# Registers in batches, a ring of twelve blocks, and other places for norms and low halves

## The chip, the cores and the metric

The kernel runs on one core of one Trainium2 chip. The time is device microseconds of one execution, as a median of several runs. The core has TensorE (PE), VectorE (DVE), ScalarE (ACT), GpSimd (POOL) and SyncE (SP, which issues most DMAs).

## The reference

x is 16 batches of 128 tokens with 256 features. Two layers, each with an attention and a feed-forward part; every part takes a layer norm of x and is added to x with a gate:

```python
x = x + tanh(g_xattn[0]) * long_conv(norm(x), k, bias, ctx, ctx)          # stage A
x = x + tanh(g_ffn[0])   * moe_and_shared(norm(x), Wr, Wg, Wu, Wd, Sg, Su, Sd, Wsg)   # stage B
x = x + tanh(g_xattn[1]) * attention_16_heads(norm(x), ctx, ctx)          # stage C, causal
x = x + tanh(g_ffn[1])   * lora_moe(norm(x), ...)                         # stage D
# stage B, for each token: p = softmax(x @ Wr); the 2 best of 8 experts, weight p
#   sum over them of p_e * (silu(x @ Wg[e]) * (x @ Wu[e])) @ Wd[e]        # width 176
#   + sigmoid(x @ Wsg) * (silu(x @ Sg) * (x @ Su)) @ Sd                   # shared, width 704
```

## The kernel before

Every engine has its own program, written out by hand in order; an engine that waits for a semaphore holds everything behind it. Products of float32 are made of three float32r products: each operand is split into a high half (a ScalarE copy to float32r) and a low half (the difference), and high*high + high*low + low*high is summed in PSUM.

**Stage B, the shared expert.** Four groups of 512 tokens, six tiles of 128 hidden units each (the last tile has 64), numbered n = 0 to 23. For tile n TensorE makes the gate and up products (`b_gate_up`, L1946, 12 matmuls), ScalarE the silu (`b_silu_of`), VectorE the product h (`b_hidden`, L1400), ScalarE and VectorE the halves of h (`b_high`, `b_low`, L1405), and TensorE adds the down product (`b_down`, L1960) one or two tiles later. Before a new group the halves of its turned x are made (`b_high_x`, `b_low_x`, L1389). At the end of each tile, `b_side` puts other work on each engine:

- the routed experts' weights come in ten chunks: SyncE fetches chunk c when the low half of chunk c - 2 is made, ScalarE makes its high half (`experts_high`, L802) in tile c, GpSimd its low half (`experts_low`, L631)
- VectorE makes the norms of groups 1 to 3 in 38 small steps, 13 per tile; ScalarE applies them in tiles 3 to 5, four batches each (`b_norm`, L762)
- TensorE turns the normed x (L1897) and makes the router's logits; VectorE takes them (`logits_copy`), picks the experts (28 steps of `route_step`, from tile 9), and writes each token's slots (L1311); then it writes the table of blocks (`table_step`)

GpSimd scatters each token's row twice into `x_d` (L635, an indirect DMA for 128 rows), so that the rows of one expert lie together: eight scatters of group 0 between the low halves, 24 after the slots of groups 1 to 3 are written.

**Stage B, the blocks.** After tile 17, 39 blocks of 128 rows are run, each with one expert. SyncE reads the block's row from the table into a register and fetches it into a ring of six buffers (`block_in`, L468 and L469), four blocks ahead; it waits until the block that had the buffer is done. SyncE's program alternates `block_in(i + 4)` and `block_out(i)` (the store to `y_d`, L473). TensorE turns the block (`blk_turn`, L1996), reads the expert's offset into a register (L2001) and makes gate and up with it as a dynamic offset (L2009), reads another register (L2023) and makes the down product (L2030), and turns h (L2019, L2020). VectorE reads a third (L1470) for the column with the weight (L1474). Per step s TensorE's order is: turn of s + 1, gate and up of s, down of s - 2, turn of h of s - 1.

**Then** come tiles 18 to 23, beside which GpSimd gathers the blocks' results back into X (L641, 32 indirect DMAs with addition, eight per group of four batches).

**Stage C.** 32 steps (half the heads of one batch each). Per step: scores (L2065, mask L2069), VectorE's row maximum (L1495) and shift (L1505) in `c_shift`, ScalarE's exp (L887), turns (L2079), values. VectorE makes the norm of a later group in 23 steps between them; `rows_complete(g)` waits until group g's gathers have landed. In the kernel before, the norm of group 1 is made ahead of the first `c_shift`, that of group g + 2 in the steps of group g; ScalarE applies the norm of g + 1 in steps 0 to 3 (`c_norm_one`, L749), TensorE turns it in steps 4 to 7.

## Time and profile before

| | us |
|---|---|
| median of 3 runs | 894.62 |
| lowest, highest | 890.34, 896.23 |
| the profiled execution | 894.95 |
| its span, first to last instruction | 893.2 |

| engine | busy us | share of the span |
|---|---|---|
| TensorE, matmuls | 724.9 | 81% |
| VectorE | 577.9 | 65% |
| ScalarE | 309.4 | 35% |
| GpSimd | 256.0 | 29% |

The mean granted clock of TensorE is 0.92 of its full 2.4 GHz. The stages in the span: A to about 172, tiles 0 to 17 to about 291, blocks to about 436, tiles 18 to 23 to about 470, C to about 631, D to the end.

### The profile page before, as it was taken

To read this page: it belongs to the slowest core of one execution; us is meant where nothing else is said; L and a number is where in the kernel's file an instruction comes from. 1 tells how busy PE (TensorE), PEld (TensorE's weight loads), DVE (VectorE), ACT (ScalarE), POOL (GpSimd) and SP (SyncE) were. 2 spreads that over 40 slices of the span, in tenths; PEclk is the share of its full clock that TensorE was granted. 3 is DMA by queue.
4 is the path that set the end of the run, shared out by engine and by line. 5 is a ranking of instruction groups with operands and counts; after the bars stand their busy time and mean duration, and the time that the engine had idled before them with its cause. 6 is when DMAs were issued, how large, how long until landed. Compare 5 with 4: busy or idle time off the path is not lost.

```text
span 893.2 us, 13171 instructions
## 1 busy us (share of the span) xinstructions
PE 724.9 (81%) x4198; PEld 574.7 (64%) x4214; DVE 577.9 (65%) x1221; ACT 309.4 (35%) x539; POOL 256.0 (29%) x256
## 2 busy tenths in 40 slices
PE   2788888587978778877874888997769899999995
PEld 2565666476767656656662555665658788788884
DVE  5879888472356444444353778889457976877764
ACT  2110110154422222222232566875334335334231
POOL 1979777454447000000076810100100000000000
PEclk9999999797979899999995789998679999999997
DMA  8210100132213222222165512120010101001000
GB/s 271 71 50 27 36 24 1 48 95 74 70 56 140 67 78 68 73 73 77 42 110 98 81 50 82 54 85 2 1 47 1 48 25 48 1 24 48 23 1 24
DMA packets 42923, 51.25 MB, mean 57 GB/s; under 512 B 7088, under 2 KB 36976, under 8 KB 42224
## 3 DMA queue, kind: packets, MB, share of 16 engines
q1 hardware_dynamic: 36720, 41.98, 14.9%
q0 software_dynamic: 6144, 8.52, 4.8%
q8 instruction: 32, 0.52, 0.2%
q14 instruction: 27, 0.22, 0.1%
HBM read 36.88 MB, written 13.59 MB: 57 GB/s over the span
## 4 chain that ended last, share of the span: by engine, by line
PE 38%; DVE 16%; DMA 10%; issue 6%; POOL 5%; ACT 5%; SPq 2%; DVEq 0%; ACTq 0%; POOLq 0%
PE bank L2158 21%; DMA A<-x_d 4%; DMA X<-y_d,A 4%; PE bank L2009 3%; PE bank L1946 3%; POOL x_d L635 3%; DVE A L1505 3%; PE bank L2079 2%; DVE small L1495 2%; POOL X L641 2%; PE bank L2030 2%; ACT A L887 2%; PE bank L1996 1%; DMA A<-rows_d 1%; PE bank L2065 1%
## 5 line engine op out<-in xcount | busy, mean ns | idle before, releaser
L2158 PE MATMUL bank<-R 128*128 128x512 f32 (+3 forms) x1080 | 221.3, 365 | 22.4 <-DVE R L1617 6.4
L2158 PEld LDWEIGHTS bank<-R 128*128 128x128 f32 (+1 forms) x1080 | 183.2, 193 | 57.8 <-issue 8.3
L641 POOL DMA_INDIRECT X<-y_d,A x32 | 50.1, 1567 | 172.6 <-DMA y_d<-A 154.6
L1946 PE MATMUL bank<-R 128*128 128x512 f32 x264 | 74.4, 438 | 5.3 <-DVE R L1389 4.3
L1946 PEld LDWEIGHTS bank<-R 128*128 128x128 f32 x264 | 55.8, 218 | 17.5 <-issue 4.4
L2079 PE MATMUL bank<-ident,A 128*128 128x128 f32 x256 | 41.4, 314 | 30.4 <-ACT A L887 30.2
L2009 PE MATMUL bank<-R 128*128 x234 | 52.2, 362 | 13.4 <-issue 13.0
L1854 PE MATMUL bank<-A 128*128 128x256 f32 x128 | 43.2, 420 | 23.6 <-issue 12.4
L586 POOL TENSOR_TENSOR A<-A 128x256 f32<-128x256 f32 x64 | 58.0, 906 | 13.7 <-DVE A L1152 13.6
L2079 PEld LDWEIGHTS bank<-ident,A 128*128 128x128 f32 x256 | 33.4, 161 | 40.0 <-ACT A L887 25.4
L697 POOL TENSOR_TENSOR A<-A 128x512 f32<-128x512 f32 x4 | 5.2, 1288 | 180.1 <-DVE A L1611 180.1
L1152 DVE TENSOR_TENSOR A<-bank,A 128x512 f32<-128x512 f32 x64 | 43.7, 683 | 16.9 <-PE bank L1856 14.4
L1400 DVE TENSOR_TENSOR A<-bank,A 128x512 f32<-128x512 f32 (+1 forms) x24 | 16.5, 689 | 58.7 <-ACT A L785 58.7
L1960 PE MATMUL bank<-R 128*128 128x256 f32 (+1 forms) x288 | 43.1, 304 | 13.7 <-DVE R L1405 13.7
L1141 DVE TENSOR_TENSOR A<-A 128x512 f32<-128x512 f32 x64 | 52.9, 827 | 2.1 <-ACT A L723 2.1
L2009 PEld LDWEIGHTS bank<-R 128*128 128x128 f32 x234 | 40.2, 201 | 21.8 <-issue 21.7
L1960 PEld LDWEIGHTS bank<-R 128*128 128x128 f32 (+1 forms) x288 | 40.3, 207 | 17.5 <-DVE R L1405 14.1
L1642 DVE TENSOR_TENSOR A<-bank,A 128x512 f32<-128x512 f32 (+1 forms) x48 | 33.0, 688 | 28.0 <-PE bank L2158 27.5
L1854 PEld LDWEIGHTS bank<-A 128*128 128x128 f32 x128 | 21.1, 197 | 42.0 <-issue 40.9
L1495 DVE TENSOR_REDUCE small<-bank 128x8 f32<-128x1024 f32 x32 | 39.0, 1219 | 14.0 <-PE bank L2069 14.0
L591 POOL TENSOR_TENSOR A<-A 128x128 f32<-128x128 f32 x64 | 43.7, 683 | 14.1 <-PE bank L1866 9.3
L681 POOL TENSOR_TENSOR R<-A,R 128x960 f32 x8 | 18.4, 2299 | 100.2 <-ACT R L882 100.2
(274 smaller groups left out, 1376.3 us busy)
## 6 DMA issues: line engine op xcount, KB each, us to landing
A<-x_d SPq DMA_DIRECT2D x39, 132.0 KB, 2.0
y_d<-A SPq DMA_DIRECT2D x39, 128.0 KB, 1.7
A<-rows_d SPq DMA_DIRECT2D x4, 1024.0 KB, 4.6
A<-in_w SPq DMA_DIRECT2D x8, 480.0 KB, 3.7
A<-in_w SPq DMA_DIRECT2D x5, 512.0 KB, 3.8
A<-in_ctx_one SPq DMA_DIRECT2D x8, 272.0 KB, 3.6
A<-in_ctx_half SPq DMA_DIRECT2D x8, 256.0 KB, 2.7
A<-in_ctx_nat SPq DMA_DIRECT2D x4, 512.0 KB, 3.7
```

The costliest lines, as they stand in the source:

```text
L586: nc.gpsimd.tensor_tensor(zh[:, u], zr[:, u, :, 0:HALF, :], zr[:, u, :, HALF:, :], ALU.add).then_inc(zh_ready, 1)
L591: nc.gpsimd.tensor_tensor(z2[:, :, :, h * I0:(h + 1) * I0], zh[:, u, :, 0:QUARTER, :], zh[:, u, :, QUARTER:, :], ALU.add).then_inc(z2_read ...
L641: nc.gpsimd.indirect_dma_start(out=X[:, b], out_offset=None, in_=y_d[:, :], in_offset=bass.IndirectOffsetOnAxis(ap=y_slots[:, b, r:r + 1], ...
L1141: nc.vector.tensor_tensor(kv[:, u], vT[:, :, t0:t0 + I0].unsqueeze(3).to_broadcast([P, 8, I0, I0]), c.unsqueeze(2).to_broadcast([P, 8, I0, ...
L1152: nc.vector.tensor_tensor(zr[:, u], yb[u].rearrange("p (q i j) -> p q i j", q=8, i=I0), c.unsqueeze(3).to_broadcast([P, 8, I0, I0]), ALU.m ...
L1495: step.mark(nc.vector.tensor_reduce(mx[:, u], S, AX_X, ALU.max))
L1854: nc.tensor.matmul(y[:, 0:n], diag, kv0, start=True, stop=False, skip_group_check=True)
L1946: mm = nc.tensor.matmul(dst, wX[:, a0:a0 + P], mX[:, k], start=(m == 0), stop=(m == 5))
L1960: mm = nc.tensor.matmul(DN[:, b * D:(b + 1) * D], hX[0:pr, n % 2, b * P:(b + 1) * P], wX[0:pr, a0:a0 + D], start=(j == 0 and m == 0 and b ...
L2009: mm = nc.tensor.matmul(GU[i % 2][:, 0:2 * EF], xX[:, i % 2, k * P:(k + 1) * P], w[:, k, :, :, bass.ds(at, RANK)], start=(m == 0), stop=(m ...
L2079: mm = nc.tensor.transpose(PTP[:, h * P:(h + 1) * P], E_[:, k % 2, h], ident[:])
L2158: mm = nc.tensor.matmul(dst, a, m, start=start and n == 0, stop=stop and n == len(prods) - 1, skip_group_check=skip)
```

## The change

- All values of the table that one engine needs in the blocks are read into registers ahead of the stage, in two loads (20 and 19 values). One table of experts, used with a factor, takes the place of three tables. The check of bounds at each read is left out.
- The ring of blocks has twelve buffers, where the rows to scatter lay before; fetches run eight blocks ahead.
- In tiles 0 to 9 VectorE makes the low halves of the routed weights. GpSimd only scatters, and begins with group 0 at once.
- VectorE finishes the norm of groups 1 to 3 in tile 2; ScalarE applies it in tiles 2 to 6, two or three batches each.
- At the end of a group the halves of h are made before those of the next x, on ScalarE and VectorE; in tile 5 the copy of the turned x comes before the silu; the logits of group 1 are taken before `b_finish`; in tile 11 no routing steps lie before the halves.
- Stage C starts without the norm of group 1. The norm of g + 1 is made in the steps of group g: from step 2 in group 0, from step 0 in the others, done in step 3. ScalarE applies it in steps 3 to 6.

```diff
@@ -72,6 +72,11 @@
 TURN_AT = (4, 5, 6, 7)
+REGS_PER_LOAD = 20
+XB = 12
+AHEAD = 8
+NORM_AT = (2, 0, 0)
+NORMS_IN = {2: (4, 5), 3: (6, 7, 8), 4: (9, 10), 5: (11, 12), 6: (13, 14, 15)}
@@ -205,7 +210,7 @@
         bsilu, bh = (A1[:, 10240 + i * 512:10240 + (i + 1) * 512].rearrange("p (u n) -> p u n", u=2) for i in range(2))
-        xb = [A1[:, 11264 + i * XROW:11264 + (i + 1) * XROW] for i in range(6)]
+        xb = [A1[:, i * XROW:(i + 1) * XROW] for i in range(XB)]
...
@@ -333,7 +339,7 @@
             sem("down_done"), sem("b_done"))
-        blk_loaded, y_stored = [sem(f"blk_loaded{i}") for i in range(6)], [sem(f"y_stored{i}") for i in range(4)]
+        blk_loaded, y_stored = [sem(f"blk_loaded{i}") for i in range(XB)], [sem(f"y_stored{i}") for i in range(4)]
@@ -378,6 +384,17 @@
+        def table_values(engine, view, top):
...
+            values = []
+            for lo in range(0, NBLK, REGS_PER_LOAD):
+                hi = min(lo + REGS_PER_LOAD, NBLK)
+                _, got = nc.values_load_multi_w_load_instructions(
+                    view[0:1, lo:hi], [engine], min_val=0, max_val=top,
+                    skip_runtime_bounds_check_because="the table's entries are bounded where it is made")
+                values.extend(got)
+            return values
@@ -456,27 +473,24 @@
                 sp.dma_start(x_d[bass.ds(at, P), :], zeros).then_inc(rows_zeroed, 16)
+            row_at = table_values(mybir.EngineType.SP, trow, X_ROWS - P)
...
             def block_in(i):
-                if i < 6:
-                    if i < 4:
-                        sp.wait_ge(xsL_ready, NCHUNK)
-                else:
-                    sp.wait_ge(y_made, i - 5)
-                at = sp.value_load(trow[0:1, i:i + 1], min_val=0, max_val=X_ROWS - P)
-                sp.dma_start(xb[i % 6], x_d[bass.ds(at, P), :]).then_inc(blk_loaded[i % 6], 16)
+                if i >= XB:
+                    sp.wait_ge(y_made, i - XB + 1)
+                sp.dma_start(xb[i % XB], x_d[bass.ds(row_at[i], P), :]).then_inc(blk_loaded[i % XB], 16)
...
             def block_out(i):
...
-            for i in range(4):
+            for i in range(AHEAD):
...
             for i in range(NBLK):
-                if i + 4 < NBLK:
-                    block_in(i + 4)
+                if i + AHEAD < NBLK:
+                    block_in(i + AHEAD)
@@ -625,11 +639,6 @@
-            def experts_low(c):
-                pool.wait_ge(xsH_ready, c + 1)
-                h, l, src = expert_chunk(c)
-                nc.gpsimd.tensor_tensor(l, src, h.bitcast(F32), ALU.subtract).then_inc(xsL_ready, 1)
@@ -643,13 +652,9 @@
-            experts_low(0)
-            experts_low(1)
-            for c in range(2, NCHUNK):
-                experts_low(c)
-                if c == 2:
-                    pool.wait_ge(slots_ready, 1)
-                scatter((c - 2) // 2, (c % 2,))
+            pool.wait_ge(slots_ready, 1)
+            for b in range(BG):
+                scatter(b)
@@ -805,9 +810,8 @@
                     experts_high(n)
-                if 3 <= n < 6:
-                    for b in range(BG):
-                        b_norm(BG * (n - 2) + b)
+                for b in NORMS_IN.get(n, ()):
+                    b_norm(b)
@@ -816,13 +820,13 @@
             def b_group(g):
...
                     n = SJ * g + j
-                    b_silu_of(n)
...
                         b_turned(1)
+                    b_silu_of(n)
+                    b_high(n - 1)
...
                         b_high_x(g + 1)
-                    b_high(n - 1)
@@ -933,10 +937,10 @@
                         c_exp(g + (k + 2) // 8, (k + 2) % 8)
-                    if more and k < BG:
-                        if k == 0:
+                    if more and 3 <= k < 3 + BG:
+                        if k == 3:
                             act.wait_ge(qT_turned, BG * (g + 1))
-                        c_norm_one(g + 1, k)
+                        c_norm_one(g + 1, k - 3)
@@ -1367,21 +1371,17 @@
                 elif i == 14:
-                    step.mark(nc.vector.tensor_scalar(tcol, te_, float(D), None, ALU.add))
+                    nc.vector.tensor_copy(tcol, te_).then_inc(table_ready, 1)
                 elif i == 15:
-                    step.mark(nc.vector.tensor_scalar(t16, te_, float(RANK), None, ALU.mult))
+                    step.mark(nc.vector.tensor_tensor(tdelta_, tcum_, tblk_, ALU.subtract))
                 elif i == 16:
-                    nc.vector.tensor_scalar(t256, te_, float(D), None, ALU.mult).then_inc(table_ready, 1)
-                elif i == 17:
-                    step.mark(nc.vector.tensor_tensor(tdelta_, tcum_, tblk_, ALU.subtract))
-                elif i == 18:
...
                 else:
-                    y_slot_step(i - 19)
+                    y_slot_step(i - 17)
...
             def block_table():
-                return Steps(table_step, 25)
+                return Steps(table_step, 23)
@@ -1425,10 +1425,21 @@
+            def experts_low(c):
+                dve.wait_ge(xsH_ready, c + 1)
+                if c >= 8:
+                    dve.wait_ge(pads_zeroed, 4)
+                h, l, src = expert_chunk(c)
+                nc.vector.tensor_tensor(l, src, h.bitcast(F32), ALU.subtract).then_inc(xsL_ready, 1)
...
             def b_side(n, norm, route, table):
+                if n == 2:
+                    norm.take_all()
                 norm.take(13)
-                if n in (6, 7, 8):
+                if n in (7, 8):
                     logits_copy(n - 5)
+                if n < NCHUNK:
+                    experts_low(n)
@@ -1438,13 +1449,13 @@
                     b_hidden(n)
-                    if j == SJ - 1 and g + 1 < G:
-                        b_low_x(g + 1)
-                    if n >= 9:
+                    if n >= 9 and j < SJ - 1:
...
                     b_low(n - 1)
+                    if j == SJ - 1 and g + 1 < G:
+                        b_low_x(g + 1)
@@ -1465,16 +1476,18 @@
+            expert = []
...
             def blk_out(i):
...
-                col = dve.value_load(tcol[0:1, i:i + 1], min_val=D, max_val=D + E - 1)
...
                     dve.wait_ge(y_stored[i % 4], 16 * (i // 4))
-                nc.vector.tensor_scalar(yo[i % 4], DB[i % 2][:, 0:D], xb[i % 6][:, bass.ds(col, 1)], None, ALU.mult
+                nc.vector.tensor_scalar(yo[i % 4], DB[i % 2][:, 0:D], xb[i % XB][:, D:].rearrange("p (e n) -> p e n", n=1)[:, bass.ds(expert[i], 1), 0], None, ALU.mult
...
             def blocks():
+                expert.extend(table_values(mybir.EngineType.DVE, tcol, E - 1))
@@ -1526,20 +1539,22 @@
             def c_steps(g, more):
                 norm = Steps()
-                if g + 2 < G:
-                    rows_complete(g + 2)
-                    norm = c_norm(BG * (g + 2), BG * (g + 3))
...
                 for k in range(8):
+                    if more and k == NORM_AT[g]:
+                        rows_complete(g + 1)
+                        norm = c_norm(BG * (g + 1), BG * (g + 2))
...
                         norm = d_norm(BG, B - BG)
-                    norm.take(3 if more else 6)
+                    norm.take((3, 3, 8, 8)[k % 4] if more and g == 0 else 3 if more else 6)
+                    if more and k == 3:
+                        norm.take_all()
@@ -1759,11 +1774,14 @@
             norm.take(8)
+            experts_low(0)
...
                     b_hidden(SJ * (g + 1))
+                if g == 0:
+                    logits_copy(1)
@@ -1783,14 +1801,9 @@
             nc.vector.memset(OT, 0.0).then_inc(ot_zeroed, 1)
-            rows_complete(1)
-            norm = c_norm(BG, 2 * BG)
-            norm.take(4)
             c_shift(0, 0)
-            norm.take(3)
-            c_shift(0, 1, norm)
-            c_shift(0, 2, norm)
-            norm.take_all()
+            c_shift(0, 1)
+            c_shift(0, 2)
@@ -1988,17 +2001,18 @@
+            expert = []
...
             def blk_turn(i):
-                pe.wait_ge(blk_loaded[i % 6], 16 * (i // 6 + 1))
+                pe.wait_ge(blk_loaded[i % XB], 16 * (i // XB + 1))
...
                 for k in range(DT):
-                    mm = nc.tensor.transpose(XT[i % 2][:, k * P:(k + 1) * P], xb[i % 6][:, k * P:(k + 1) * P],
+                    mm = nc.tensor.transpose(XT[i % 2][:, k * P:(k + 1) * P], xb[i % XB][:, k * P:(k + 1) * P],
...
             def blk_gate_up(i):
-                at = pe.value_load(t16[0:1, i:i + 1], min_val=0, max_val=(E - 1) * RANK)
@@ -2007,7 +2021,7 @@
                         mm = nc.tensor.matmul(GU[i % 2][:, 0:2 * EF], xX[:, i % 2, k * P:(k + 1) * P],
-                                              w[:, k, :, :, bass.ds(at, RANK)], start=(m == 0), stop=(m == 5))
+                                              w[:, k, :, :, bass.ds(expert[i] * RANK, RANK)], start=(m == 0), stop=(m == 5))
@@ -2020,7 +2034,6 @@
             def blk_down(i):
-                at = pe.value_load(t256[0:1, i:i + 1], min_val=0, max_val=(E - 1) * D)
@@ -2028,12 +2041,14 @@
                         mm = nc.tensor.matmul(DB[i % 2][:, 0:D], hX[:, i % 2, a0:a0 + P],
-                                              w[:, bass.ds(at, D)], start=(m == 0), stop=(m == 5))
+                                              w[:, bass.ds(expert[i] * D, D)], start=(m == 0), stop=(m == 5))
...
             def blocks():
                 pe.wait_ge(table_ready, 1)
+                pe.wait_ge(xsL_ready, NCHUNK)
+                expert.extend(table_values(mybir.EngineType.PE, tcol, E - 1))
```

## Rows read from the trace of the kernel before

**Rows 1.** Stretches of the span: us, busy by engine, TensorE's clock, DMA share, GB/s.

```profile
172.00:255.00 83.00, 65.91 (x338) 56.77 (x338) 40.93 (x103) 38.88 (x59) 34.47 (x26) 0.83 0.25 77
...
292.00:299.00 7.00, 5.91 (x21) 5.07 (x22) 1.62 (x4) 1.79 (x5) 0.00 (x0) 0.52 0.29 77
299.00:436.00 137.00, 107.37 (x600) 83.33 (x599) 61.30 (x151) 39.35 (x112) 0.00 (x0) 0.97 0.23 70
```

**Rows 2.** Timeline of TensorE, tiles: start, us, instruction, idle before.

```profile
196.41 2.73 PE L1960 MATMUL bank<-R 128*128 128x256 f32 x12 [2.65 <-DVE R L1405]
...
207.17 2.93 PE L1960 MATMUL bank<-R 128*128 128x256 f32 x12 [3.65 <-DVE R L1405]
...
218.27 1.94 PE L1897 MATMUL bank<-ident,A 128*128 128x128 f32 x8 [1.95 <-DVE A L1247]
...
247.51 0.22 PE L1916 MATMUL bank<-A 128*128 128x96 bf16 x1 [2.11 <-DVE A L1273]
...
275.23 1.60 PE L1960 MATMUL bank<-R 128*128 128x256 f32 x12
...
279.41 1.60 PE L1960 MATMUL bank<-R 128*128 128x256 f32 x12
```

**Rows 3.** One line's durations (min/median/max ns), then timeline of GpSimd and VectorE.

```profile
L1087 DVE TENSOR_TENSOR A<-A x3: 170/172/2785, 191.5 to 196.5; 128x12 f32<-128x12 f32 x3
...
192.54 2.37 POOL L631 TENSOR_TENSOR R<-A,R 128x1024 fp32r<-128x1024 f32 x1
...
195.67 0.68 DVE L1405 TENSOR_TENSOR R<-A,R 128x512 fp32r<-128x512 f32 x1
```

**Rows 4.** Slots written, the scatters by line, the first block's turn.

```profile
254.48 0.18 DVE L1311 CAST A<-A 128x24 int32<-128x24 f32 x1
...
L635 POOL DMA_INDIRECT x_d<-A x32: 959/964/2449, 191.3 to 286.7; - x32
...
292.07 0.52 PE L1996 MATMUL bank<-ident,A 128*128 128x128 f32 x2 [3.15 <-DMA A<-x_d]
```

**Rows 5.** Timeline of TensorE in the blocks, gate products.

```profile
294.30 2.12 PE L2009 MATMUL bank<-R 128*128 x6 [0.37 <-issue]
...
299.09 1.25 PE L2009 MATMUL bank<-R 128*128 x6
...
301.57 1.27 PE L2009 MATMUL bank<-R 128*128 x6
...
430.03 1.26 PE L2009 MATMUL bank<-R 128*128 x6 [0.25 <-issue]
```

**Rows 6.** Register loads by line: all, then one of 416:418; timeline of TensorE.

```profile
L2001 PEldq TENSOR_LOAD <-A x39: 296/302/563, 293.2 to 429.2; - x39
...
L2023 PEldq TENSOR_LOAD <-A x1: 303/303/303, 417.1 to 417.1; - x1
...
416.70 1.27 PE L2009 MATMUL bank<-R 128*128 x6 [0.41 <-issue]
```

**Rows 7.** Waits of 300:430: total us, times, longest.

```profile
PE bank L1996 <- DMA A<-x_d: 12.3, 17, 1.4
```

**Rows 8.** Timeline at the attention: first scores, then VectorE.

```profile
472.99 0.63 PE L2069 MATMUL bank<-neg,identb 128*128 128x512 bf16 x1 [0.33 <-issue]
...
483.31 1.41 DVE L1062 BATCH_NORM_STATS2 A<-X 128x6 f32<-128x256 f32 x4 [13.02 <-DMA X<-y_d,A]
...
498.82 1.08 DVE L1062 BATCH_NORM_STATS2 A<-X 128x6 f32<-128x256 f32 x3 [0.32 <-DMA X<-y_d,A]
...
499.82 1.21 DVE L1495 TENSOR_REDUCE small<-bank 128x8 f32<-128x1024 f32 x1
...
537.82 1.21 DVE L1495 TENSOR_REDUCE small<-bank 128x8 f32<-128x1024 f32 x1
...
571.26 1.22 DVE L1495 TENSOR_REDUCE small<-bank 128x8 f32<-128x1024 f32 x1
...
602.73 1.19 DVE L1495 TENSOR_REDUCE small<-bank 128x8 f32<-128x1024 f32 x1
```

11 lines of the change are left out of this document (6 added, 5 removed).

## The prediction

> **What bounds the kernel now.** I read the table of stretches first [rows 1]. TensorE is busy nearly all of the last stage, which the change doesn't touch. Three stretches leave room. In 172 to 255 (tiles 0 to 11 of the shared expert) its granted clock is 0.83 of 2.4 GHz on average. In 299 to 436 (39 blocks) TensorE is busy 107 of 137 us at 0.97. At 470 the attention starts late.
>
> The timeline of the tiles [rows 2] shows TensorE waiting for VectorE before the down products of tiles 2 and 4, before the turn of group 2's rows and before the ranks: 2.65 + 3.65 + 1.95 + 2.11 = 10.4 us. A tile without waits takes 4.18 (275.23 to 279.41). One reason lies in [rows 3]: a step of the norm on 128x12 values took 2.79 us where the same line takes 0.17 at other times, and GpSimd's low half of 2.37 us ran from 192.54 beside it.
>
> What ends the tiles isn't TensorE. The last slots are written at 254.66; then GpSimd issues 24 scatters until 287.66, 1.36 us apart on average; the last lands, the first block is fetched, and its turn starts at 292.07 after a wait of 3.15 [rows 4]. So what counts here is when the slots are ready; the 37.4 us behind them are one queue.
>
> In the blocks [rows 5] the gate products start 294.30, 299.09 (two later), 301.57, and last 430.03: 38 intervals in 135.7 us, 3.57 each, while the interval 299.09 to 301.57 is 2.48. The waits [rows 7] name 12.3 us before the turns for the fetch. Another part is the register load: TensorE's queue takes 0.30 us to read a value, twice per block [rows 6].
>
> In the attention VectorE sat 13.02 us until 483.31 for the gathered rows of group 1, though the first scores were there at 473.6, and the fourth reduction came at 499.82 after a second wait for group 2, which ended at 498.82 [rows 8].
>
> **The tiles.** Ten low halves go from GpSimd (2.37 us each) to VectorE. VectorE's own difference of 128x512 takes 0.68 [rows 3], so one of 128x1024 is about 1.2, and ten are 11.6 us (nine of 1.2, one of 0.68; the trace shows none of this size on VectorE; at the rate of the 0.68 row the bounds are 1.1 and 1.36 each). They stand at the end of a tile's VectorE work, where it has some 2 us of slack against a tile of 4.18, except where norm steps stand too. I followed the queues with the durations of the trace:
> - The 10.4 us of TensorE's waits go, with two causes: GpSimd no longer stops VectorE, and the halves of h come before the halves of x.
> - Waits come back: 1.0 before the down of tile 0 (a low half in front of the second hidden tile), 1.5 before that of tile 2 (ScalarE now waits for the whole norm in tile 2 with the next silu queued behind it), 2.3 before that of tile 4 (norms 9 and 10 and the copy of the turned x stand ahead of the silu). Sum 4.8. Net 5.6.
> - With fewer gaps some of the 1.2 GHz stretches end. At 0.83 over 83 us about 14 us were at the low level, which costs up to 7 us of TensorE time if it is all in matmuls; I take 3.4, half.
> So the slots are ready 9.0 us earlier (between 4, if a wait more is left and the clock stays, and 13). The chain of chunk loads (fetch waits for a low half two chunks back, then the high half, then the low half) takes about 1.2 + 4 + 1.1 us in two tiles of 4.2 and stays hidden; if it didn't, each tile would cost 1 to 2 us.
>
> The 24 scatters keep their 33 us. The eight of group 0 now come before, beside the first tiles, and hold nobody. SyncE's registers for the fetches are read while it waits for the scatters, 0.5 us off the path (its first value was read between the last landing and the fetch). The zeroing of pads, 15 transfers, waits for the table, which moves earlier with the tiles and is then done 5 to 10 us ahead of the scatters. Tiles 12 to 17 end before the scatters, so the changes there give nothing. First block 9.5 us earlier. TensorE then idles longer before it, and starts at 1.2 GHz as now (0.52 in 292 to 299), which I keep.
>
> The Trainium skill, "GPSIMD Engine Reference" (Specifications), says that GpSimd's SBUF interfaces are shared with VectorE, with contention when VectorE has two SBUF inputs. By that rule, the trace agrees [rows 3], and it also speaks against the change: the low halves have two such inputs and now lie beside the eight early scatters. By the rule those would be late by up to 10 us, in a stretch where nothing waits for them, so the sum stays.
>
> **The blocks.** Per block three register loads go (two on TensorE's queue, one each on VectorE's and SyncE's) and are replaced by two batches per engine ahead of the stage; those on TensorE and SyncE stand in front of waits that last anyway, VectorE's stand before the first low half of a block, while the scatters still run. I cost them at nothing; no row shows a load of 20 registers, and if 39 values last as 39 single ones (39 x 0.30 = 11.7 us), VectorE, which has some 7 idle before the first block, costs 5, so 0 to 5. The load of 20 is nearer to one instruction, so I take 0.
> The ring of twelve with fetches eight ahead asks for a block that ended three blocks ago; a fetch takes 2.1 us plus issue, and no wait remains. What is left is the array: gate products 1.25, down products about 0.83, four turns of 0.11 apart. That is the 2.48 of [rows 5], of which there is only one sample. Dependences: from the turn of h over ScalarE (0.38) and VectorE (0.43) to the down product are 1.3 us, where the turn and gate products of the next block give 1.7. ScalarE's 1.1 and VectorE's 1.7 us of work in a block don't bind. I take 2.52 (bounds 2.48, and 2.9, the interval of undelayed blocks now). First two intervals 4.8 as before, 36 x 2.52 = 90.7, and 2 for stretches at half clock: 97.5 against 135.7, gain 38.2 (with 2.9: 24.6; with no half clock and 2.48: 41.6).
>
> The Trainium skill, "TensorE: Matmul & The Clock Gate" (Step-by-step), says that the sequencer spends about 62 ns on each matmul. What TensorE's queue did is seen in [rows 6]: gate products began at 416.70, and the next register load started at 417.1, with twelve instructions (weight loads and matmuls) between: some 33 ns each. At 62 ns for weight loads and matmuls alike, a block of 32 would be 2.0 us plus address operations and waits of 0.6, so an interval of 2.6 and 3 us less gain. The trace doesn't agree, and I stay with 2.52.
>
> **The attention.** The norm of group 1 leaves the start. The first reduction can begin at 473.6 and not 484.6, 11.0 earlier, and the fourth no longer waits for group 2: 1.4 more. Rows of group 1 land at 483.3, when VectorE reaches them after some 487; group 2 at 498.7 against 505 or later; group 3 some 20 us early. So none of these waits is due. Put back: from the fourth reduction of a group to that of the next were 33.4 us with a norm of a later group inside and 31.5 without [rows 8]; the last group now gets one: 2.0. ScalarE's norms wait in step 3 for the end of VectorE's steps, in group 0 for eleven of them, 2.2 us with 1 of cover; next is the copy of turned p: 1.2. Net 9.2, bounds 4 and 12.4.
>
> **Sum.** The profiled execution took 894.95 (span 893.2 and 1.75 around); the median is 894.62, the same within 0.04%. 894.95 - 9.5 - 38.2 - 9.2 = 838.
>
> **Rivals.**
> A. The blocks stay near 2.9 because a dependence or the queue's order binds and not the load: gain 24.6 there, 852. For it: only one interval of 2.48. Against: the 1.3 against 1.7 above. Chance 0.18.
> B. The tiles give nothing, since VectorE's 11.6 us take what GpSimd's stalls cost: 838 + 9 = 847. Chance 0.12.
> C. Norm steps inside the attention are exposed one by one (23 steps of 0.2 in each of three groups, 14 us): 838 + 9 = 847. Chance 0.1.
> D. Slower: the longer idle before the blocks holds TensorE at 1.2 GHz through them. At that clock an interval is up to 2 x 2.48 = 4.96, 2.44 over mine. The gain of 56.9 is gone when 23 of 38 intervals are so; all of them give 838 + 93 = 931. For it: the clock was 0.52 in 292 to 299 and the tiles of 172 to 255 ran at 0.83. Against: it rose after 7 us, and the blocks will have fewer gaps than those that ran at 0.97. Chance 0.03.
> E. The change doesn't do what it says: fetches or loads still hold the blocks (a batch that stands in the way, or a fetch queued behind a store): 850 to 862. Chance 0.07.
> The forecast itself: 0.5.
>
> **Range.** The corners of the bounds are 829 and 864; 827 to 856 leaves out most of E, D and the worst corner. A measurement tells about 1% from no change, 9 us. Faster by over 1%: 0.95; within 1%: 0.01; slower: 0.04.
>
> **What would show it.** Starts of the gate products 2.5 apart with no wait for a fetch; no small norm step of over 2 us in the tiles; slots ready about 245.5 and the first turn about 282.5, still one queue of scatters between; the first reduction of the attention some 3 us after its memset and no wait for a gather of over 2 us after it. The prediction is wrong if VectorE becomes what tiles wait for, if intervals of blocks stay over 2.8, or if TensorE's clock in the blocks is under 0.9.

## The result, and the profile after

The changed kernel took 825.07 us in the median of four runs (817.5 to 830.01) beside 892.94 for the kernel before (890.34 to 896.23): a ratio of 0.921, 95% interval 0.912 to 0.930. The ratios here leave out the few executions that ran in the chip's slower state, among them the one of 830.01. The profiled execution took 828.8 (span 827.1, mean clock 0.928), 66.1 us under the 894.95 of before; 838 was forecast.

Where the 66.1 us come from, by the starts of the same instructions in both traces: 12.9 until the first block's turn (forecast 9.5; 0.5 of it lies ahead of the tiles); 50.8 from there to the last block's gate products (38.2); 1.8 from there to the last reduction of the attention (9.2); 0.6 behind it.

Stretches of the changed kernel (us, busy time by engine, TensorE's clock, DMA share, GB/s), to be held against [rows 1]:

```profile
172.00:255.00 83.00, 71.45 (x416) 61.52 (x417) 54.85 (x142) 41.32 (x64) 20.93 (x25) 0.96 0.29 92
...
299.00:360.00 61.00, 61.00 (x435) 57.91 (x434) 42.81 (x109) 26.48 (x82) 0.00 (x0) 1.00 0.40 117
```

In the tiles the clock is 0.96 where it was 0.83; in the blocks TensorE is never shown idle, at full clock.

The tiles and the queue behind them, from timelines of TensorE and GpSimd, against [rows 2, 4]:

```profile
185.84 1.67 PE L1973 MATMUL bank<-R 128*128 128x256 f32 x12 [0.99 <-DVE R L1405]
...
195.96 1.70 PE L1973 MATMUL bank<-R 128*128 128x256 f32 x12 [1.45 <-DVE R L1405]
...
203.23 1.70 PE L1973 MATMUL bank<-R 128*128 128x256 f32 x12 [1.88 <-DVE R L1405]
...
235.02 0.22 PE L1929 MATMUL bank<-A 128*128 128x96 bf16 x1 [2.66 <-DVE A L1277]
...
242.20 1.15 POOL L644 DMA_INDIRECT x_d<-A  x1 [56.87 <-DVE A L1315]
...
279.22 1.09 PE L2011 MATMUL bank<-ident,A 128*128 128x128 f32 x4 [10.06 <-DMA A<-x_d]
```

Three waits before down products are 0.99, 1.45 and 1.88, as followed (1.0, 1.5, 2.3); the fourth, before the ranks, didn't go (2.66, was 2.11). The scatters start at 242.20, were 254.93, and their queue is as long as before.

One block of the changed kernel, all engines (timeline, weight loads left out):

```profile
292.14 1.23 PE L2023 MATMUL bank<-R 128*128 x6
292.20 0.38 ACT L852 ACTIVATE R<-bank 128x256 fp32r<-128x256 f32 x1 [0.75 <-PE bank L2034]
...
292.62 0.42 DVE L1476 TENSOR_TENSOR R<-bank,R 128x256 fp32r<-128x256 f32 x1
...
293.21 0.62 PE L2043 MATMUL bank<-R 128*128 x3
...
294.02 0.27 PE L2033 MATMUL bank<-ident,A 128*128 128x128 f32 x1
...
294.24 0.38 PE L2011 MATMUL bank<-ident,A 128*128 128x128 f32 x2
...
294.37 0.41 PE L2023 MATMUL bank<-R 128*128 x1
```

The interval is 2.23 here (292.14 to 294.37) and 2.24 over the stage; the first starts are 280.97, 283.17 and 285.39, the last 366.36, against [rows 5]. The busy time of the six gate products is 1.23, yet the down products begin 1.07 after them: the busy time holds the tail of the last matmul, beneath which the next ones already start.

The batches of register loads (one line, by queue: count, min/median/max ns, first and last start), where [rows 6] had one load per value:

```profile
L392 SPq TENSOR_LOAD <-A x2: 4566/4704/4842, 263.8 to 268.6; - x2
L392 PEldq TENSOR_LOAD <-A x2: 4928/5435/5942, 267.6 to 273.6; - x2
L392 DVEq TENSOR_LOAD <-A x2: 4441/4915/5389, 269.2 to 274.6; - x2
```

A batch of 20 or 19 values lasts 4.4 to 5.9 us, 0.24 to 0.28 a value over both, little less than the 0.30 of a single load [rows 6]. They are hidden: SyncE's end at 273.2, ahead of the last landing of the scatters at 276.7; TensorE's second begins at 273.6, and as the pair of durations fits only with the longer one first, it ends at 278.5, 0.7 before the turn.

In the attention the reductions (L1508) stand at 408.47 (484.63 before), 423.02, 460.93, 498.79 and 535.95 for the first and the fourth of each group, against [rows 8]; the last is at 557.32 (622.77 before). The start came 76 us earlier, of which groups 1 to 3 gave back 11.4. The chain of waits in steps 5 and 6 of group 0 shows with what:

```profile
450.85 1.06 ACT A L891
451.90 0.49 ACT A L754
...
452.44 0.44 PE bank L2125 x2
452.88 0.87 PE bank L2094 x8
```

After the exponential (L891) ScalarE computes a norm (L754), TensorE turns the normed rows (L2125), and only then p (L2094). Three steps in a row with this link are 4.08 to 4.13 us apart; in the kernel before the steps at the same place are 3.49, 3.87 and 3.49 apart.

### The profile page after: what moved, and what is told of

It is laid out like the page before. It is cut to its first block, busy times and chain, and to the rows that moved or that the text cites. A ratio compares the mean times of both kernels' runs of the same rounds, so it can differ in the third digit from the quotient of the medians.

```text
span 827.1 us, 12725 instructions
## 1 busy us (share of the span) xinstructions
PE 699.6 (85%) x4214; PEld 564.3 (68%) x4214; DVE 577.7 (70%) x1229; ACT 306.2 (37%) x539; POOL 233.1 (28%) x246
## 4 chain that ended last, share of the span: by engine, by line
PE 49%; DVE 16%; ACT 6%; issue 5%; POOL 3%; DMA 2%; DVEq 0%; ACTq 0%; SPq 0%
PE bank L2173 22%; PE bank L2023 5%; PE bank L2043 4%; PE bank L1959 4%; POOL x_d L644 3%; PE bank L2094 3%; PE bank L2080 2%; DVE A L1518 2%; DVE small L1508 2%; ACT A L891 2%; PE bank L2105 1%; PE bank L1973 1%; DVE A L1066 1%; DMA A<-rows_d 1%; PE bank L2011 1%
## 5 line engine op out<-in xcount | busy, mean ns | idle before, releaser
L2173 PEld LDWEIGHTS bank<-R 128*128 128x128 f32 (+1 forms) x1080 | 183.4, 193 | 56.9 <-issue 7.4
L650 POOL DMA_INDIRECT X<-y_d,A x32 | 50.3, 1571 | 119.0 <-DMA y_d<-A 101.8
L1959 PE MATMUL bank<-R 128*128 128x512 f32 x264 | 66.7, 404 | 5.3 <-DVE R L1389 4.3
L600 POOL TENSOR_TENSOR A<-A 128x256 f32<-128x256 f32 x64 | 58.8, 919 | 12.4 <-DVE A L1156 12.3
L1959 PEld LDWEIGHTS bank<-R 128*128 128x128 f32 x264 | 50.0, 195 | 15.5 <-issue 4.4
L1508 DVE TENSOR_REDUCE small<-bank 128x8 f32<-128x1024 f32 x32 | 39.1, 1220 | 28.2 <-PE bank L2084 28.2
L2094 PE MATMUL bank<-ident,A 128*128 128x128 f32 x256 | 41.8, 317 | 13.3 <-ACT A L891 13.3
L644 POOL DMA_INDIRECT x_d<-A x32 | 34.1, 1065 | 66.2 <-DVE A L1315 56.9
L1657 DVE TENSOR_TENSOR A<-bank,A 128x512 f32<-128x512 f32 (+1 forms) x48 | 33.0, 688 | 28.0 <-PE bank L2173 27.6
L2023 PE MATMUL bank<-R 128*128 x234 | 50.2, 353 | 0.7 <-DVE R L1464 0.7
L1867 PEld LDWEIGHTS bank<-A 128*128 128x128 f32 x128 | 20.6, 193 | 42.2 <-issue 41.4
L2094 PEld LDWEIGHTS bank<-ident,A 128*128 128x128 f32 x256 | 35.2, 165 | 20.8 <-ACT A L891 17.7
L993 ACT ACTIVATE A<-bank 128x512 f32<-128x512 f32 (+1 forms) x48 | 28.6, 595 | 52.8 <-PE bank L2173 52.6
L686 POOL TENSOR_TENSOR R<-A,R 128x960 f32 x8 | 18.4, 2299 | 100.6 <-ACT R L886 100.6
L1973 PE MATMUL bank<-R 128*128 128x256 f32 (+1 forms) x288 | 39.4, 286 | 7.6 <-DVE R L1405 7.5
L2080 PE MATMUL bank<-A 32*128 32x256 f32 x256 | 43.8, 467 | 2.1 <-issue 2.1
```

The lines of the kernel that those rows point to most:

```text
L600: nc.gpsimd.tensor_tensor(zh[:, u], zr[:, u, :, 0:HALF, :], zr[:, u, :, HALF:, :], ALU.add).then_inc(zh_ready, 1)
L644: nc.gpsimd.indirect_dma_start(out=x_d[:, :], out_offset=bass.IndirectOffsetOnAxis(ap=slots[:, b, r:r + 1], axis=0), in_=row_of(b), in_off ...
L650: nc.gpsimd.indirect_dma_start(out=X[:, b], out_offset=None, in_=y_d[:, :], in_offset=bass.IndirectOffsetOnAxis(ap=y_slots[:, b, r:r + 1], ...
L1508: step.mark(nc.vector.tensor_reduce(mx[:, u], S, AX_X, ALU.max))
L1867: nc.tensor.matmul(y[:, 0:n], diag, kv0, start=True, stop=False, skip_group_check=True)
L1959: mm = nc.tensor.matmul(dst, wX[:, a0:a0 + P], mX[:, k], start=(m == 0), stop=(m == 5))
```

## The experiments

Thirteen runs, each of two to six executions. "Blocks" is the time from the start of the first gate product of the first block to that of the last gate product of the last block (136.7 before, 86.3 after); an interval is the distance between the first gate products of two blocks in a row. For the attention three times are given: from the last gate product to the fourth reduction, then from there to that of group 1, and from that to the last reduction of all. Ratios are to the kernel before as run beside each, with 95% intervals (its medians were 889.23 to 894.8).

| kernel | median us | ratio | blocks | attention |
|---|---|---|---|---|
| before | 892.94 | | 136.7 | 68.8, 38.0, 85.0 |
| changed | 825.07 | 0.921 (0.912, 0.930) | 86.3 | 55.7, 37.9, 96.4 |
| changed_again | 826.26 | 0.928 (0.923, 0.933) | 86.3 | 56.0, 43.2, 93.6 |
| attention_old | 822.33 | 0.925 (0.920, 0.930) | 86.5 | 65.5, 37.0, 84.7 |
| attention_mixed | 814.31 | 0.915 (0.911, 0.920) | 86.4 | 55.3, 42.4, 84.8 |
| low_on_gpsimd | 830.38 | 0.934 (0.929, 0.940) | 86.8 | |
| ring_of_six | 851.02 | 0.959 (0.953, 0.966) | 104.7 | |
| load_per_block | 853.44 | 0.958 (0.951, 0.966) | 108.1 | |
| four_gate_products | 828.24 | 0.932 (0.924, 0.940) | 85.1 | |
| mixed_and_vector_low | 816.8 | 0.917 (0.912, 0.922) | 86.3 | 55.9, 42.2, 85.0 |
| low_wait_late_four | 813.0 | 0.911 (0.907, 0.915) | 69.7 | |
| low_wait_late | 825.98 | 0.924 (0.919, 0.928) | 82.5 | |
| halves_as_before | 834.51 | 0.936 (0.932, 0.941) | 86.2 | |
| norms_together | 829.67 | 0.928 (0.923, 0.933) | 86.4 | |
| mixed_and_late_wait | 813.1 | 0.910 (0.906, 0.914) | 82.4 | 53.4, 44.7, 84.6 |

The ratios of changed_again and of the changed kernel in the first row differ by 0.7 points: that is how much two groups of runs of the same kernel can differ.

### The blocks: fetches and loads

**changed_again**, the changed kernel beside the others.

> The changed kernel itself, so that the variants of this call have a measure on the same chip. Expected: 820 to 828 us, gate products of the blocks 2.24 apart, steps of the attention 4.13 apart where ScalarE's norm lies in front of a turn.

**ring_of_six.**

```diff
-XB = 12
-AHEAD = 8
+XB = 6
+AHEAD = 4
```

> The changed kernel with a ring of six buffers and fetches four blocks ahead, registers still read in batches. Theory 1 (the ring alone has a price of its own): a fetch is issued when block i is done and stored, 0.4 us, lands 2.1 later and is due two steps on, which asks for steps of about 2.7 us; intervals of 2.65 to 2.85, time 16 to 23 us above the changed kernel. Theory 2 (the register loads were what made fetches late, so a ring of six is enough without them): intervals of 2.24 to 2.3, within 4 us.

24.8 us slower than the changed kernel, somewhat over theory 1; 18.4 us of it lie in the blocks, an interval of 2.73. The chain of waits repeats this every 5.45 us, two blocks:

```profile
324.96 0.50 DVE A L1486
...
325.48 0.33 SPq L487
...
325.99 2.07 DMA A<-x_d
...
328.11 0.44 PE bank L2011 x2
328.55 1.04 PE bank L2023 x6
329.58 0.72 PE bank L2043 x6
```

VectorE scales the output (L1486), SyncE stores it (L487), only then issues the next fetch, which lands after 2.07; then turn, gate and down products lead to the next output. Between them the fetch and its place in SyncE's queue are a ring of two blocks. With eight ahead it is slack: in the changed kernel no turn after the first waits for a fetch.

**load_per_block.** The batches are gone; each engine reads its value in the block that uses it (one table of experts, so an address operation more than before).

```diff
-                expert.extend(table_values(mybir.EngineType.PE, tcol, E - 1))
...
             def blk_gate_up(i):
+                at = pe.value_load(tcol[0:1, i:i + 1], min_val=0, max_val=E - 1)
...
             def blk_down(i):
+                at = pe.value_load(tcol[0:1, i:i + 1], min_val=0, max_val=E - 1)
```

> The changed kernel with a register load per use again on TensorE, VectorE and SyncE, but the ring of twelve. Theory 1 (my step of 2.48 for the array held hidden load time; TensorE's queue is what binds with loads): intervals of 2.7 to 2.9 with no wait for a fetch, 18 to 25 us above the changed kernel. Theory 2 (loads are hidden under matmuls once no fetch is late): intervals of 2.24 to 2.48, 0 to 9 us above.

27.2 us slower, 21.8 of it in the blocks, an interval of 2.8 to 2.9, also a little over theory 1. TensorE's timeline:

```profile
327.69 1.27 PE L2023 MATMUL bank<-R 128*128 x6 [0.15 <-issue]
329.01 0.63 PE L2044 MATMUL bank<-R 128*128 x3
...
330.62 0.43 PE L2023 MATMUL bank<-R 128*128 x1 [0.18 <-issue]
```

In this block, from gate to down products are 1.32 in place of 1.07, and from there to the next gate products 1.61 in place of 1.16. Of these 0.70 us only 0.15 and 0.18 are shown as idle: the rest lies beneath the tails of matmuls that count as busy. Taken back alone, the ring costs 18.4 and the loads cost 21.8, which is 40.2 of the 50.4 us won in the blocks. So the two gains overlap: some 10.2 us are there as soon as either of the two is made, and are lost only when both are taken back.

### The blocks: what is left

**four_gate_products** leaves out the two products with the low half of x in each block's gate and up.

```diff
-                for xX, wX in ((bxH, guH), (bxH, guL), (bxL, guH)):
+                for xX, wX in ((bxH, guH), (bxH, guL)):
```

> The changed kernel without the products of the low half of x in the blocks' gate and up (four matmuls of six; that part of the sum is left out). Theory 1 (the array sets the interval of 2.24): 2 x 0.18 less, 1.88, 14 us faster. Theory 2 (the way of h over ScalarE and VectorE to the down product sets it): the interval stays above 2.1.

The interval stayed at 2.24 in this stretch (2.23 over the stage), so the array alone doesn't set it. The timeline (all engines, weight loads left out):

```profile
291.51 0.91 PE L2023 MATMUL bank<-R 128*128 x4
291.57 0.39 ACT L852 ACTIVATE R<-bank 128x256 fp32r<-128x256 f32 x1 [1.07 <-PE bank L2034]
...
291.99 0.42 DVE L1476 TENSOR_TENSOR R<-bank,R 128x256 fp32r<-128x256 f32 x1
...
292.57 0.63 PE L2043 MATMUL bank<-R 128*128 x3 [0.15 <-DVE R L1476]
...
293.51 0.27 PE L2034 MATMUL bank<-ident,A 128*128 128x128 f32 x1
...
293.81 0.38 ACT L852 ACTIVATE R<-bank 128x256 fp32r<-128x256 f32 x1 [1.04 <-PE bank L2034]
```

A ring: the turned h is copied (291.57), its low half made (291.99), the down products wait for it (292.57), the next h is turned behind them (293.51) and copied at 293.81, which is 2.24 after 291.57. The order of TensorE's queue closes it: turn h(i+1) stands behind down(i).

**low_wait_late_four and low_wait_late** cut that ring: the last two of six down products alone need the low half, and the wait is moved to stand in front of them.

```diff
             def blk_down(i):
-                pe.wait_ge(bhL_ready, i + 1)
+                pe.wait_ge(bhH_ready, i + 1)
...
                 for hX, w0_, w1_ in ((bhH, dH0, dH1), (bhH, dL0, dL1), (bhL, dH0, dH1)):
+                    if hX is bhL:
+                        pe.wait_ge(bhL_ready, i + 1)
```

> The changed kernel, but the down products wait for h's low half only before the last two of their six (the first four need the high half alone), and the gate and up products of a block leave out the two with the low half of x. With four gate products and the wait ahead of all six down products the interval stayed at 2.24 us. Theory 1 (a ring holds it there: copy of the turned h on ScalarE 0.39, low half on VectorE 0.43, down products and the next turn of h 1.0 to 1.2, with 0.15 to 0.2 between): with the wait later the ring is some 0.5 us shorter, TensorE alone is left, and the interval falls by the two products, 2 x 0.18, to 1.88 (gain 13 us in 38 intervals). Theory 2 (something outside that ring, a fetch or VectorE's turn with the output, gives the beat): the interval stays at 2.24.

> The changed kernel with that later wait alone, all twelve products there. Theory 1 (TensorE's own work, 1.08 for the gate products, 0.81 for the down products and 0.35 for four turns, is 2.24 as well, so that ring and engine are level): interval 2.24, time within 2 us of the changed kernel. Theory 2 (the ring alone gave 2.24 and TensorE's own work is less): the interval falls to 2.1 or below, 5 us or more faster.

With four gate products the interval falls to 1.81 and the time by some 15 us: theory 1. The chain is TensorE alone:

```profile
327.69 0.67 PE bank L2023 x4
328.36 0.71 PE bank L2045 x6
329.07 0.11 PE bank L2033
329.18 0.11 PE bank L2034
329.29 0.22 PE bank L2011 x2
```

With all twelve products the interval is 2.15 (gate products at 327.42 and 329.57), so the engine alone needs 0.09 less than the ring held it to. That is between the two theories: the interval lies nearer to the second (2.1) than to the first (2.24), while the median, 0.3 us under that of changed_again, is as the first has it. The 3.8 us that the trace shows in the blocks are too few for the medians to tell.

### The tiles

**low_on_gpsimd** gives the ten low halves back to GpSimd, in the old order among the scatters.

```diff
+            for c in range(2, NCHUNK):
+                experts_low(c)
...
-                if n < NCHUNK:
-                    experts_low(n)
```

> The changed kernel with the low halves of the routed weights back on GpSimd and everything else of the change kept. Theory 1 (the two engines hold each other up): steps of the norm of over 2 us come back, the whole norm is late, ScalarE waits for it in tile 2, slots ready 3 to 6 us later than in the changed kernel, time 3 to 6 us above it, since the scatters set the start of the blocks. Theory 2 (the reordered halves of h gave the gain of the tiles): within 1.5 us of the changed kernel.

**halves_as_before.** ScalarE's side of the end of a group; VectorE's likewise. The routing steps and, in tile 5, the silu stand in the old order too.

```diff
-                    b_high(n - 1)
                     if j == SJ - 1 and g + 1 < G:
                         act.wait_ge(gu_ready, n + 1)
                         b_high_x(g + 1)
+                    b_high(n - 1)
```

> The changed kernel, but in the shared expert's tiles ScalarE and VectorE make the halves of x for the next group ahead of those of h again, the routing steps stand in the last tile of a group as before, and the silu stands ahead of the copy of the turned rows. Low halves on VectorE and spread norms stay. Theory 1 (the order was one of the two causes of TensorE's waits, 2.65 us before the down products of tile 2 and 3.65 before those of tile 4 in the kernel before): waits of 2 to 4 us return before the down products at the ends of the groups, and the slots are ready 3 to 6 us later. Theory 2 (what was won came from GpSimd's low halves and from the spread norms): the slots are ready within 1 us of the changed kernel's.

**norms_together.**

```diff
-                for b in NORMS_IN.get(n, ()):
-                    b_norm(b)
+                if 3 <= n < 6:
+                    for b in range(BG):
+                        b_norm(BG * (n - 2) + b)
...
-                if n == 2:
-                    norm.take_all()
```

> The changed kernel, but the twelve norms of ScalarE stand in tiles 3, 4 and 5 in fours as before, and VectorE takes 13 norm steps per tile without finishing them in tile 2. Theory 1 (the norms were a part of the waits: four of them, some 2 us, ahead of ScalarE's next silu): the waits before the down products of tiles 3 to 5 grow to 2 to 4 us each in place of 1.0, 1.5 and 1.9, the slots are ready 3 to 5 us later. Theory 2 (in the tiles the spread norms give nothing, since VectorE must now end its steps in tile 2): the slots are ready within 1 us, or earlier.

The traces are compared from the start of the 36 gate products of the first tiles (174.50 before, 174.03 after), in us to the first late scatter and to the first block's turn: before 80.4 and 117.6; changed 68.2 and 105.2; changed_again 67.4 and 103.9; low_on_gpsimd 68.8 and 105.7; halves_as_before 69.7 and 110.8; norms_together 69.0 and 105.6. Against the mean of the two changed runs each part undone alone puts the slots 1.0, 1.9 and 1.2 later, in each case under the 3 us and more of theory 1. That is 4.1 of 12.6. The other 8.5 either stay as long as some of the parts are there or belong to one that no run takes back (the logits of group 1, taken earlier); no run takes two parts back together, so this stays open. In norms_together the waits of TensorE in question are 1.11 and 2.71, where theory 1 had 2 to 4 each. (The 4.1 us by which the median of low_on_gpsimd is slower meets its theory 1, but only 1.1 of it is there at the first turn.)

What the three don't give back is the low clock: in 172 to 255 it is 0.83 before, 0.96 in the changed kernel, and 0.94, 0.92 and 0.94 with one part undone. In the order of halves the waits did return (3.21 and 3.48 before down products), and the table comes late enough that the batches stand on the path. The chain of waits:

```profile
267.93 4.86 SPq L392
272.82 4.04 SPq L392
277.09 2.06 DMA A<-x_d
279.16 2.60 issue
281.76 0.68 PE bank L2011 x2
```

SyncE's two loads hold the first fetch until 277.09, and TensorE's own, the second of which starts at 277.1, hold the turn 2.60 longer. So the first turn comes 6.2 later with slots only 1.9 later, most of the 7.5 us that the ratios show.

In low_on_gpsimd a step of the norm was held again. GpSimd and VectorE beside each other (timeline):

```profile
186.51 2.40 POOL L645 TENSOR_TENSOR R<-A,R 128x1024 fp32r<-128x1024 f32 x1 [1.30 <-ACT R L816]
186.65 2.28 DVE L1088 TENSOR_SCALAR A<-A 128x12 int32<-128x12 int32 x1
```

The small step ends with GpSimd's operation: 188.93 and 188.91. A second one, of 2.25 us, ends at 229.68 with GpSimd's at 229.56. The step of 2.79 us in [rows 3] was of this kind (it ended at 194.95, GpSimd's operation at 194.91), and it was one of three in the tiles of the kernel before: the others took 2.38 from 188.72 and 2.25 from 240.80. With two of the three back, the slots were only 1.0 later.

### The attention

**attention_old** has the order of the kernel before there, all else changed.

```diff
+            rows_complete(1)
+            norm = c_norm(BG, 2 * BG)
...
-                    if more and k == NORM_AT[g]:
-                        rows_complete(g + 1)
-                        norm = c_norm(BG * (g + 1), BG * (g + 2))
...
-                    if more and 3 <= k < 3 + BG:
+                    if more and k < BG:
```

> The changed kernel with the attention's schedule as before (norm of group 1 first, norm of group g + 2 in the steps of group g, ScalarE's norms in steps 0 to 3). Theory 1 (the new places of ScalarE's norms and turns cost nearly what the early start gives, 12.9 us won and 11.4 lost): 1 to 3 us slower than the changed kernel, with 33 and 31.5 us between fourth reductions of groups 1 to 2 and 2 to 3 instead of 37.9 and 37.2. Theory 2 (the longer groups come from TensorE's clock or the DMAs of that execution and not from the schedule): 10 to 13 us slower than the changed kernel, with 37 to 38 us per group in both.

3.9 us faster in the median, with intervals of the ratios that overlap: the new order of the attention gives nothing, and perhaps costs. The groups are those of theory 1 (33.2 and 31.5 us for groups 1 and 2), but it had expected a slower kernel. The start is 10 us later and the groups behind group 0 are 84.7 in place of 93.6 to 96.4. The three times add up to 187.2, against 192.8 in changed_again and 190.0 in the changed kernel's own trace; the two differ by group 0 above all (43.2 and 37.9), for a reason that comes below.

**attention_mixed** keeps the early start and puts the norms back where they are cheap.

```diff
+                    if g == 0 and k == 2:
+                        rows_complete(1)
+                        norm = c_norm(BG, 2 * BG)
+                    if g == 0 and k == 5:
+                        rows_complete(2)
+                        norm = c_norm(2 * BG, 3 * BG)
+                    if g == 1 and k == 0:
+                        rows_complete(3)
+                        norm = c_norm(3 * BG, 4 * BG)
...
+                    at = 3 if g == 0 else 0
+                    if more and at <= k < at + BG:
```

> The changed kernel with the late norm of group 1 kept, but the norm of group 2 begun in step 5 of group 0 and ScalarE's norms of groups 2 and 3 in steps 0 to 3, away from the turns of q in steps 4 to 7. Theory 1 (ScalarE's norm, 0.50 us, is in the ring of exp, norm, turn of q, turn of p, copy when it lies in the same steps as the turn): 8 to 10 us faster than the changed kernel, 811 to 818 us, groups of 33.4 and 31.5. Theory 2 (VectorE's norm steps or the clock make the groups long): within 3 us of the changed kernel.

12 us faster than changed_again; the later groups took 84.8 again. The run moves VectorE's norms as well as ScalarE's, so it shows what the order costs, and not which of the two engines makes it so.

Two causes beside the link over ScalarE can be read from the traces. Group 2 took 37.2 us in the changed kernel at a clock of 0.91, 35.5 in changed_again at 1.00 and 31.5 in attention_mixed at 1.00. So 1.7 us go with the lower clock of one execution, and 4.0 with the order. Of these 4.0 the three steps with the link over ScalarE give 1.5. The others lie in the steps ahead of them, where the chain of waits holds VectorE's norm too (changed_again):

```profile
509.34 0.99 DVE A L1093
...
510.35 0.17 DVE A L1088
```

Group 0 took 42.4, though, and one step of VectorE in it shows why in part:

```profile
446.63 4.99 POOL L686 TENSOR_TENSOR R<-A,R 128x960 f32 x2
...
447.88 3.78 DVE L1513 TENSOR_SCALAR small<-small 128x8 f32<-128x8 f32 x1
```

The step on 128x8 values, 0.17 us elsewhere, ends at 451.66, GpSimd's pair of low halves at 451.62.

**mixed_and_vector_low** makes those low halves on VectorE too.

```diff
-                for r in range(2):
-                    split_low1(g, r)
...
+                        nc.vector.tensor_tensor(w1L[:, n * W1C:(n + 1) * W1C], stg1[k // 4],
```

> The kernel with the mixed attention schedule, and the eight low halves of the last stage's weights (128x960) on VectorE in steps 2 and 6 of each group, not on GpSimd. Theory 1 (a low half on GpSimd stops VectorE for up to 3.8 us in a step, and the gap drops TensorE's clock): no VectorE step of over 2 us in the attention, groups 1 to 4 us shorter in spite of 1.15 us more per half on VectorE, 2 to 8 us faster than the mixed schedule. Theory 2 (VectorE is in the ring of every step, and 9.2 us more work costs as much as the stalls): within 3 us of it, or slower.

No small step is held, and nothing is won: 816.8, group 0 42.2. VectorE pays for the low halves itself.

**mixed_and_late_wait** joins the edit of attention_mixed with the later wait in the blocks.

> The changed kernel with the mixed order of the attention's norms (the time 814.31 us alone) and the later wait for h's low half in the blocks (an interval of 2.15 in place of 2.24 us). Theory 1 (the two are apart, and the 42.4 us that group 0 of the attention took in the profile of the mixed order were the 3.8 us step of VectorE beside GpSimd's low halves, which falls differently when the stage begins 3 us earlier): the blocks give 3.4 us, 811 us in the median; group 0 takes 38 to 39 us if no small step of VectorE takes over 2 us, and over 41 only where one does. Theory 2 (the mixed order itself makes group 0 long, and its gain is in the later groups alone): group 0 takes over 41 us without any such step, and the median is still 811 to 815.

813.1 us, the fastest full kernel, 1.8 points of the ratio under changed_again; the blocks took 82.4. Group 0 took 44.7 with a held step:

```profile
438.00 4.97 POOL L686 TENSOR_TENSOR R<-A,R 128x960 f32 x2
...
438.78 4.23 DVE L1513 TENSOR_SCALAR small<-small 128x8 f32<-128x8 f32 x1
```

The changed kernel itself took 37.9 in group 0 without such a step and 43.2 with one of 3.18 (443.20 to 446.38, where GpSimd's operation ran to 446.35). The other runs with the order of the changed kernel say the same: with held steps of this kind of 1.62, 2.39, 3.04, 4.51 and 4.60 us group 0 took 39.1, 39.7, 41.7, 44.3 and 44.6, and with 0.8 or less 38.2, 37.8 and 37.8 (in the order low_on_gpsimd, norms_together, four_gate_products, load_per_block, low_wait_late; ring_of_six, low_wait_late_four, halves_as_before). So the step accounts for most of it, as theory 1 has it. The 42.2 of mixed_and_vector_low had none; two low halves on VectorE explain some 2.4 of that, an estimate by the 1.21 us that one of 128x1024 takes. What the mixed order by itself does to group 0 stays open.

## Why the prediction was off

The direction and the places were right, and all three terms were mis-sized: the blocks gave 12.6 us more than forecast and the tiles 3.4 more, the attention gave 7.4 less. That the total is off by only 9.2 in the profiled execution is luck, as the errors partly cancel. The median fell 2 us under the range of 827 to 856; the profiled 828.8 lies in it, and changed_again's median of 826.26 just under it. By the prediction's own bounds the corners are 827.5 and 861.9 (866.9 with the batches' 5), and not 829 and 864.

**The blocks: 50.3 against 38.2 between the gate products, the step that failed.** The forecast took the array as what is left, which is nearly so, but it mis-sized its work. It took "gate products 1.25, down products about 0.83, four turns of 0.11 apart" for it, 2.52 us a block; the starts give 2.14. Busy times of pipelined groups hold a tail that the next group hides. TensorE's timeline of before had the answer in the starts:

```profile
299.09 1.25 PE L2009 MATMUL bank<-R 128*128 x6
300.17 0.52 PE L2030 MATMUL bank<-R 128*128 x3
...
300.89 0.27 PE L2019 MATMUL bank<-ident,A 128*128 128x128 f32 x1
...
301.10 0.38 PE L1996 MATMUL bank<-ident,A 128*128 128x128 f32 x2
```

1.08 + 0.72 + 0.21 and 0.13 for the turn of x (294.24 to 294.37 after) are 2.14; low_wait_late measured 2.15. The sample of 2.48 was no measure of the array: between 301.10 and the gate products at 301.57 are 0.47, so it had a register load in it, which the forecast both counted as gone and kept in the sample. The ring over ScalarE and VectorE was looked at and dismissed ("1.3 us, where the turn and gate products of the next block give 1.7"). The 1.7 holds the same tail: from the turn of h at 294.02 to the down products at 295.45 are 1.43, and the way over the two engines, whose low half ends at 295.28, takes as long. So the ring binds at 2.24, and cost 3.8 us. The 12.1 us between the gate products are then 36 x 0.27 = 9.8 for the interval, 2.0 for half clock that wasn't needed (0.50 in 281 to 285, 1.00 from 285 to 367) and 0.4 for the first two intervals (4.4 in place of 4.8). Rival A (2.9) fell: no interval is so long once both the loads and the short ring are gone. The interval of 2.6 worked out in the prediction for 62 ns on weight loads and matmuls alike didn't come: in the chain of low_wait_late_four the two turns of h, a weight load and a matmul each, are 0.11 apart, 55 ns an instruction. The Trainium skill, "TensorE: Matmul & The Clock Gate" (Step-by-step), gives the 62 ns for matmuls, and only where the hardware decoder is off, which no run here tells; the trace doesn't agree that weight loads cost as much, and for matmuls alone it doesn't tell.

**The batches: cost nothing, for another reason.** "The load of 20 is nearer to one instruction" is wrong: 39 values take 9.4 to 10.9 us, near the pessimistic end of 11.7. They are hidden since the tables are ready early, on TensorE by only 0.7 us; with halves_as_before the cover is gone, and they hold the first block.

**The tiles: 12.9 against 9.5, mis-sized.** The waits that come back were 0.99, 1.45 and 1.88 as followed; that before the ranks stayed. So the waits gave some 3.4 net (10.4 less 7.0) and not 5.6. The clock gave more: "at 0.83 over 83 us about 14 us were at the low level" takes the time lost for the stretch at the low level. With half speed there, a mean of 0.83 is 28 us at the low level and 14 lost; at 0.96 it is 3.3 lost. Up to 10.8 could come back, where 3.4 was taken. That the clock gave the rest is worked out and not shown by a run of its own: the slots came 12.2 earlier after the start of the tiles, of which the waits explain 3.4, and the twelve down products that took 2.73 and 2.93 us behind the long waits [rows 2] took 1.67 to 1.70 after. Rival B (the tiles give nothing) fell: low halves of 128x1024 take 1.21 on VectorE, as estimated.

The Trainium skill, "GPSIMD Engine Reference" (Specifications), says that the interfaces to SBUF are shared with VectorE and that instructions in a 2-port mode or with two SBUF inputs contend. The traces agree, with more in them: a held step on 128x8 or 128x12 values lasts until GpSimd's operation ends, to within 0.04 us in five of the cases above. Whether the held steps with one input in SBUF run in a 2-port mode, no trace here shows. The prediction feared up to 10 us for the eight early scatters. Only one of them lay beside a low half on VectorE: it took 1.03 us in the changed kernel and 1.53 in changed_again, where 0.96 is usual.

**The attention: 1.8 against 9.2, mis-sized.** The start gave 13.1 (from the last gate product to the fourth reduction 68.8 and 55.7; forecast 12.4). Put back were 11.4 in the groups, not 3.2. The forecast priced "ScalarE's norms wait in step 3" once; it didn't see that in steps 3 to 6 they lie between the exponential and the turn of p each time: groups 1 and 2 took 37.9 and 37.2 us between their fourth reductions, where [rows 8] have 33.4 and 31.5. attention_old and attention_mixed show that the order does it; that the norms of ScalarE have a part is read from the chain of waits (1.5 us of the 4.0 in group 2 of changed_again). Rival C, VectorE's norm steps, was right for another part: they stand on the chain in the steps before, at times held by GpSimd. Rivals D and E didn't occur: the clock in the blocks is 1.00 after their first 4 us, and no fetch after the first was waited for.

## What to carry to other kernels

To see what a stage would take without its waits, add the distances between starts in the timeline and not the busy times, and look for the ring through the other engines that closes behind the engine's own queue. When a wait covers several matmuls, put it before the first that needs it. A step moved to hide one wait has to be priced in every iteration it then stands in, on each engine that passes it on.

## What the runs showed of the hardware

A register load of 20 or 19 values takes 4.4 to 5.9 us in the changed kernel, 0.24 to 0.28 a value beside 0.30 for a single one: batching saves little per value, and pays by its place. A step of VectorE on a few values in SBUF (TENSOR_SCALAR or TENSOR_TENSOR), 0.17 us by itself, lasted up to 4.6 us when GpSimd's elementwise operation ran beside it, in five traces through two of these in a row (4.97 to 5.0 us), while steps that read PSUM beside the same operation (445.85 to 448.65 in the changed kernel) took their usual 1.23 (445.32 and 447.93). Whether a step falls into such a stretch changes from one run to the next with the same code (37.9 and 43.2 us for group 0), so differences of a few us in the attention need several profiles.
